# Gate and up products of a routed feed-forward: the token rows are held and the weights are moved, and the activations are transposed afterwards

## The chip, the cores and the metric

The kernel runs on one core of a Trainium2 chip. Its engines work side by side: TensorE (PE, matrix products, with its weight loads listed as PEld), VectorE (DVE), ScalarE (ACT), GpSimd (POOL) and SyncE (SP), which only issues transfers here. They hand work to each other by semaphores. The metric is the device time of one execution in microseconds (us), lower is better.

## The reference

Tokens `x` (32 batches of 112 rows of 256) first get a gated cross-attention over a context. The part that matters here comes after it, a mixture of eight experts with two chosen for each token:

```python
x = x + jnp.tanh(g_xattn[0]) * attention(...)
h = layernorm(x)
bids = jax.nn.sigmoid(h @ conf_w.T + conf_b) * wealth
top_bids, chosen = jax.lax.top_k(bids, 2)            # 2 of 8 experts
combine = sum(one_hot(chosen) * softmax(top_bids)[..., None], axis=2)
def ffn(gw, uw, dw):                                  # gw, uw 1024x256, dw 256x1024
    g = h @ gw.T
    u = h @ uw.T
    return (silu(g) * u) @ dw.T
out = x + jnp.tanh(g_ffn[0]) * einsum("ebsh,bse->bsh", all_ffn(h), combine)
```

The products have to be near fp32 precision. The kernel splits each fp32 operand into a high and a low fp16 part, and forms hi\*hi, hi\*lo and lo\*hi, so that each logical product is three passes of fp16.

## The kernel before

**Stages.** Until about 880 us the program does the attention for all batches, and routes: each token's normalised row is scattered twice, once for each chosen expert, into `routed_rows` in DRAM, which is sorted by expert. The second stage takes this table in tiles of P = 128 rows. There are NT = 63 tiles; a table `t_exp_i`, computed on VectorE after tile 0, gives the expert's place for each tile. Everything this case touches is in the second stage.

**One tile.** `xt` (128 rows x 256) is loaded by GpSimd's queue (`load_tile`, line 547), transposed by TensorE into `xP` (`tile_T`, line 1558), and split into `xT` high (ACT, `tile_hi`, line 842) and low (DVE, `tile_lo`, line 1302). Gate and up have 1024 outputs each, done in two halves i = 0, 1 of 512. `gate_up(t, q, i, slot)` forms `gP[i]` and `uP[i]` (one PSUM bank each). In the kernel before, each half of each of the two is four blocks of 128 outputs; a block is a `product` (line 1383, the helper that issues all fp16 products) of KD = 2 depth blocks by three parts, six matmuls. In each the *weights* are the stationary operand (128x128) and the *rows* `xT` move (128 columns). So the outputs come out with the features on the partitions, ready to be the stationary operand of the next product, and one bank takes 24 matmuls and 24 weight loads.

ACT then forms `sg` = silu(gate) (`silu`, line 848), DVE `act_h` = up \* constant \* sg (`gated`, line 1308), ACT the high part `aT[..][0]` (`act_hi`, line 854) and DVE the low part `aT[..][1]` (`act_lo`, line 1313). `down(t)` holds `aT` and moves the down weights in 256 columns, 24 matmuls into `yP`; DVE scales the rows (`weigh`, line 1320) into `ysb`, and GpSimd adds them to the output by a scattering, accumulating DMA (`add_tile`, line 598).

**Order of the work.** It is written out by hand in one `step(t, k)` for each engine, and each engine keeps its order:

- TensorE: `gate_up(t, 0)`, `tile_T(t + 1)`, on one tile in five `expert_sums`, `gate_up(t, 1)`, then a register load of the next tile's place (`place_of`), `down(t - 1)`, and the waits for the next tile's weights.
- ACT: `silu(t, 0)`, `act_hi(t, 0)`, `tile_hi(t + 1)`, `silu(t, 1)`, `act_hi(t, 1)`, then work on a later expert.
- DVE: `gated(t, 0)`, `act_lo(t, 0)`, `tile_lo(t + 1)`, `gated(t, 1)`, `act_lo(t, 1)`, `weigh(t - 1)`, then work on a later expert.
- GpSimd: waits until the add of tile t - 2 has landed, loads `xt` of tile t + 2, then adds tile t - 1.

The work on later experts belongs to tiles 0 to 34, five for each expert p = 1 to 7: in the first three ACT squares two pieces of 1024 raw weight columns each (`expert_squares`, line 796), in the last two ACT and DVE split three pieces each into high and low (`expert_hi` line 806, `expert_lo` line 1167). In the fourth, DVE also computes the expert's scale in a chain of small operations, with a power on GpSimd within it (lines 1149 to 1162). GpSimd loads the raw pieces in `load_raw` (line 510). Four expert slots lie in SBUF as `W2`; places 4 to 7 are split into a fifth, stored to DRAM by ACT's queue (line 812) and reloaded by SP's (line 397) when a slot is free.

The slot of a tile is a register from tile 3 on: `weights_of(byte, ...)` addresses `W2` by that register plus a constant. In tiles 0 to 2 the byte is a Python constant. The semaphore `s_there` tells TensorE that a slot is loaded; for the first four places SP raises it by hand, in the kernel before at line 410, behind its last transfers of the first stage.

Of the kernel before, what the change touches and what calls it, by code (L numbers as in the profile page):

```python
# [11 lines left out]
ACT = mybir.ActivationFunctionType  # L12
# [42 lines left out]
AHEAD = 4  # L55
assert AHEAD * P * E <= 2 * (TOK - 8 * S)
RELOADS = 4
X_TOP = 2.0 ** 10
A_TOP = 2.0 ** -21
SPAN = 5  # L60
# [21 lines left out]
def build(nc, x, ctxt, mask, scal, lnw, wqkv, wout, confw, confbw, wffn, out):  # L82
# [4 lines left out]
    with ctx:  # L87
        def sem(name):
            return ctx.enter_context(nc.semaphore(name))
# [4 lines left out]
        def psum(name, shape, stack):  # L94
            return stack.enter_context(nc.psum_tensor(name, shape, F32))
# [153 lines left out]
        yP = psum("yP", [P, 2, D], ppb)[:, 0, :]  # L249
        bP = psum("bP", [P, 512], ppb)  # L250
        uP = [psum(f"uP{i}", [P, 512], ppb) for i in range(2)]
        ppb.close()
        pb.close()

# [34 lines left out]
        s_xt = [sem(f"s_xt{i}") for i in range(4)]  # L289
        s_xtp, s_xthi, s_xtlo, s_gu, s_silu, s_act = [sem(n) for n in (  # L290
            "s_xtp", "s_xthi", "s_xtlo", "s_gu", "s_silu", "s_act")]
        s_athi, s_atlo, s_down, s_yw, s_add = [sem(n) for n in (
            "s_athi", "s_atlo", "s_down", "s_yw", "s_add")]

        def need(eng, semaphore, count):

# [11 lines left out]
        def seq(b, n):  # L308

            if isinstance(b, int) and b > B - 3 and n >= PK:  # L310
                n -= KD
            return b * NPIECE + (PRO + n)

        def zseq(b, k):

            return k if isinstance(b, int) and b == 0 else seq(b - 2, PZ + k)

        def in_place(p):

# [13 lines left out]
        def _(sp):  # L333
# [38 lines left out]
            def load_raw(p):  # L372

                e = sp.value_load(order_i[0:1, p:p + 1], min_val=0, max_val=E - 1)
                for c in range(PIECES):
                    need(sp, s_wlo, (p - 1) * PIECES + c + 1)
                    sp.dma_start(raw[:, piece_cols(c)],  # L377
                                 wffn[bass.ds(e, 1), :, piece_cols(c)].rearrange("a p c -> (a p) c")).then_inc(s_raw[c], 16)

            for b in range(8):  # L380
                turn_of(b, b % 2)
            with sp.Fori(4, B // 2) as g:
# [24 lines left out]
            load_raw(1)  # L407
            turn_of(B + 4, 0)

            sp.sem_inc(s_there, 16 * RELOADS * SLOTS)  # L410
            sp.wait_ge(s_tab, 1)
            for n in range(SLOTS, E):

# [218 lines left out]
        def _(act):  # L632
# [211 lines left out]
            def silu(t, i, place):  # L844

                act.wait_ge(s_gu, t * 2 + (i + 1))
                need(act, s_act, (t - 1) * 2 + (i + 1))
                nc.scalar.activation(sg[i][:, :], gP[i][:, :], ACT.Silu, scale=constant(place, 0)).then_inc(s_silu, 1)  # L848

            def act_hi(t, q, i):  # L850

                act.wait_ge(s_act, t * 2 + (i + 1))
                need(act, s_down, t)
                nc.scalar.activation(aT[q][i][:, 0, :, :].rearrange("p m s -> p (m s)"), act_h[i][:, :], ACT.Copy).then_inc(s_athi, 1)  # L854

            def step(t, k):
                q = k % 2
                if t < NT:
                    if t == 3:
                        act.wait_ge(s_tab, 1)  # L860
                    place = place_of(t)
                    silu(t, 0, place)
                    act_hi(t, q, 0)
                if t < NT - 1:
                    tile_hi(t + 1, 1 - q)
                if t < NT:
                    silu(t, 1, place)
                    act_hi(t, q, 1)
                p, j = t // SPAN + 1, t % SPAN
                if p < E:  # L870
                    if j < 3:
                        for c in (2 * j, 2 * j + 1):
                            expert_squares(p, c)
                    else:
                        for c in range((j - 3) * 3, (j - 2) * 3):
                            expert_hi(p, c)
                if SLOTS < p <= E and j == 0:
                    put_place(p - 1)

            tile_hi(0, 0)  # L880
            for t in range(NT):
                step(t, t % 4)

        @block.vector
        def _(dve):
# [419 lines left out]
            def gated(t, i, place):  # L1305

                dve.wait_ge(s_silu, t * 2 + (i + 1))
                nc.vector.scalar_tensor_tensor(out=act_h[i][:, :], in0=uP[i][:, :], scalar=constant(place, 2), in1=sg[i][:, :],  # L1308
                                               op0=ALU.mult, op1=ALU.mult).then_inc(s_act, 1)

            def act_lo(t, q, i):
                dve.wait_ge(s_athi, t * 2 + (i + 1))
                nc.vector.tensor_tensor(aT[q][i][:, 1, :, :].rearrange("p m s -> p (m s)"), act_h[i][:, :],  # L1313
                                        aT[q][i][:, 0, :, :].rearrange("p m s -> p (m s)"), ALU.subtract).then_inc(s_atlo, 1)

            def weigh(t, k, place):
# [5 lines left out]
            def step(t, k, place, last_place):  # L1322
                q = k % 2
                p, j = t // SPAN + 1, t % SPAN
                if t < NT:
                    gated(t, 0, place)
                    act_lo(t, q, 0)
                if t < NT - 1:
                    tile_lo(t + 1, 1 - q)
                if p < E and j == 3:  # L1330
                    expert_bound(p, bP)
                if t < NT:
                    gated(t, 1, place)
                    act_lo(t, q, 1)
                if p < E and j == 3:
                    expert_scale(p)
                if t > 0:
                    weigh(t - 1, (k - 1) % 4, last_place)
                if p < E and j >= 3:
                    for c in range((j - 3) * 3, (j - 2) * 3):  # L1340
                        expert_lo(p, c)
# [34 lines left out]
        def _(pe):  # L1376
# [194 lines left out]
            def gate_up(t, q, i, slot_):  # L1571

                if i == 0:
                    pe.wait_ge(s_xtlo, t + 1)
                need(pe, s_act, (t - 1) * 2 + (i + 1))
                for o, w in ((gP[i], WG), (uP[i], WU)):
                    for m in range(IB // 2):
                        col = w + (i * (IB // 2) + m) * P
                        last = product(o[:, m * P:(m + 1) * P], lambda k, a: weights_of(slot_, a, col + k * I, P),
                                       lambda k, a: xT[q][:, a, k, :], KD)  # L1580
                last.then_inc(s_gu, 1)

            def down(t, q, slot_):

# [14 lines left out]
            def step(t, k, byte, last_byte):  # L1599

                q = k % 2
                if t < NT:
                    gate_up(t, q, 0, byte)
                if t < NT - 1:
                    tile_T(t + 1, (k + 1) % 4)
                if t // SPAN + 1 < E and t % SPAN == 3:
                    expert_sums(t // SPAN + 1, bP)
                if t < NT:
                    gate_up(t, q, 1, byte)
                place = next_byte = None  # L1610
                if t == 2:
                    pe.wait_ge(s_tab, 1)
                if t < NT - 1:
                    place = place_of(t + 1)
                    next_byte = byte_of(place)
                if t > 0:
                    down(t - 1, 1 - q, last_byte)
                if t < NT - 1:
                    weights_there(place)
                return next_byte  # L1620
# [44 lines left out]
```

## Time and profile before

| | |
|---|---|
| median of 3 runs | 1584.86 us (1583.99 to 1586.45) |
| profiled execution, own time | 1586.34 us |
| profiled execution, span of the trace | 1584.7 us |
| mean granted TensorE clock | 0.984 |
| busy: PE, PEld, DVE, ACT, POOL | 91%, 69%, 66%, 59%, 30% |
| second stage, first gate product to the last down product | 880.74 to 1572.39 us |

The span is the time from the first to the last instruction of the trace, and the execution's own time has a little around it. The busy share of PE counts the time in which at least one matmul is under way. Matmuls are pipelined, so that the duration of one tells its latency and not its rate: a rate is read from the start of a run of matmuls to the start of the next run. In a row of the timeline, "x24" is 24 instructions merged, and the bracket tells how long the engine sat idle before, and for what ("issue" is an idle time that no semaphore in the profile explains).

### The profile page before, as it was taken

To read this page: it belongs to the slowest core of one execution; us is meant where nothing else is said; L and a number is where in the kernel's file an instruction comes from. 1 tells how busy PE (TensorE), PEld (TensorE's weight loads), DVE (VectorE), ACT (ScalarE), POOL (GpSimd) and SP (SyncE) were. 2 spreads that over 40 slices of the span, in tenths; PEclk is the share of its full clock that TensorE was granted. 3 is DMA by queue.
4 is the path that set the end of the run, shared out by engine and by line. 5 is a ranking of instruction groups with operands and counts; after the bars stand their busy time and mean duration, and the time that the engine had idled before them with its cause. 6 is when DMAs were issued, how large, how long until landed. Compare 5 with 4: busy or idle time off the path is not lost. (4 is left out here: it accounts for less than half of the span.)

```text
span 1584.7 us, 46877 instructions
## 1 busy us (share of the span) xinstructions
PE 1439.6 (91%) x15896; PEld 1096.9 (69%) x15896; DVE 1046.5 (66%) x2552; ACT 942.0 (59%) x1940; POOL 475.9 (30%) x644
## 2 busy tenths in 40 slices
PE   1999999999999999999996799999998999999996
PEld 1566666666666666666665788888787888888875
DVE  4688898898988989889877555445435533333332
ACT  4678777787878778787867454545445422222221
POOL 4232224334243342432413332233222212212211
PEclk9999999999999999999996899999999999999999
DMA  3011011111111010110122542333357231111351
GB/s 114 18 38 38 27 38 42 44 36 50 37 39 50 27 58 24 50 45 29 38 93 75 160 108 38 93 108 120 89 184 237 52 105 26 26 28 26 105 187 15
DMA packets 52198, 107.49 MB, mean 68 GB/s; under 512 B 10704, under 2 KB 32592, under 8 KB 51472
## 3 DMA queue, kind: packets, MB, share of 16 engines
q0 software_dynamic: 20448, 43.13, 11.4%
q1 hardware_dynamic: 29824, 46.70, 9.8%
q10 hardware_dynamic: 1712, 14.70, 2.5%
q8 instruction: 148, 2.42, 0.6%
q14 instruction: 66, 0.54, 0.1%
HBM read 69.16 MB, written 35.34 MB: 66 GB/s over the span
## 5 line engine op out<-in xcount | busy, mean ns | idle before, releaser
L1308 DVE SCALAR_TENSOR_TENSOR act_h<-uP,consts,sg 128x512 f32<-128x512 f32 x126 | 94.6, 751 | 253.0 <-ACT sg L848 252.7
L848 ACT ACTIVATE sg<-gP,consts 128x512 f32<-128x512 f32 x126 | 86.5, 687 | 280.1 <-PE uP L1383 280.0
L1383 PE MATMUL uP<-xT,W 128*128 128x128 f16 x3024 | 250.0, 217 | 0.9
L1383 PE MATMUL fP<-zTs,ws 128*128 128x112 f16 (+1 forms) x1536 | 221.2, 295 | 10.5 <-POOL zTs L479 8.9
L1383 PEld LDWEIGHTS uP<-xT,W 128*128 (+1 forms) x3024 | 209.5, 96 | 29.5 <-issue 4.7
L1383 PE MATMUL gP<-xT,W 128*128 128x128 f16 x3024 | 223.7, 218 | 5.6 <-DVE xT L1302 3.2
L1383 PE MATMUL yP<-W,aT 128*128 (+1 forms) x1512 | 179.3, 275 | 44.8 <-issue 43.9
L1383 PEld LDWEIGHTS gP<-xT,W 128*128 (+1 forms) x3024 | 202.1, 97 | 22.6 <-issue 7.9
L1383 PEld LDWEIGHTS yP<-W,aT 128*128 128x128 f16 x1512 | 144.4, 98 | 71.4 <-issue 52.8
L598 POOL DMA_INDIRECT out<-ysb,xt x63 | 105.2, 1669 | 287.9 <-DVE ysb L1320 266.6
L702 ACT ACTIVATE pr<-ms,nmax 112x488 f32<-112x488 f32 x256 | 179.0, 699 | 15.9 <-DVE nmax L948 14.3
L1383 PE MATMUL fP<-ws,zTs 128*128 128x512 f16 x768 | 187.0, 379 | 0.2
L948 DVE CUSTOM_DVE_ANT_0 ms<-simP,madd,sim_undo 112x488 f32<-112x488 f32 x256 | 184.1, 719 | 3.1 <-PE simP L1431 0.8
L1383 PEld LDWEIGHTS fP<-zTs,ws 128*128 128x128 f16 x1536 | 110.0, 99 | 102.2 <-issue 38.1
L954 DVE SCALAR_TENSOR_TENSOR pT<-ptP,pT 122x448 f16<-122x448 f32 x256 | 158.0, 617 | 20.9 <-ACT pT L709 19.9
L709 ACT ACTIVATE pT<-ptP 122x448 f16<-122x448 f32 x256 | 137.8, 538 | 39.9 <-PE ptP L1441 38.6
L1383 PE MATMUL oP<-v,pT 122*128 122x64 f16 x3072 | 133.5, 194 | 20.4 <-DVE pT L954 17.6
L854 ACT ACTIVATE aT<-act_h 128x512 f16<-128x512 f32 x126 | 79.3, 630 | 118.3 <-DVE act_h L1308 118.3
L1313 DVE TENSOR_TENSOR aT<-act_h,aT 128x512 f16<-128x512 f32 x126 | 87.2, 692 | 87.7 <-ACT aT L854 87.7
L1441 PE MATMUL ptP<-ident,pr 112*122 112x112 f32 x1024 | 142.6, 262 | 0.5 <-DVE filled L1059 0.5
L1383 PEld LDWEIGHTS oP<-v,pT 122*128 122x128 f16 x3072 | 122.7, 98 | 28.9 <-DVE pT L954 28.8
L1441 PEld LDWEIGHTS ptP<-ident,pr 112*122 112x122 f32 x1024 | 115.2, 140 | 25.2 <-issue 1.2
(210 smaller groups left out, 2119.0 us busy)
## 6 DMA issues: line engine op xcount, KB each, us to landing
raw<-wffn POOLq DMA_DIRECT2D x36, 512.0 KB, 7.2
split_experts<-W ACTq DMA_DIRECT2D x4, 3072.0 KB, 10.4
W<-split_experts SPq DMA_DIRECT2D x16, 768.0 KB, 8.0
xc<-ctxt SPq DMA_DIRECT2D x32, 375.0 KB
xt<-routed_rows POOLq DMA_DIRECT2D x63, 129.0 KB, 2.4
raw<-wffn SPq DMA_DIRECT2D x12, 512.0 KB, 9.0
xl<-x SPq DMA_DIRECT2D x32, 112.0 KB
xres<-x SPq DMA_DIRECT2D x32, 112.0 KB, 4.8
```

The lines of the kernel that those rows point to most:

```text
L598: pool.indirect_dma_start(out[:, :], bass.IndirectOffsetOnAxis(ap=xt[k][:, D:D + 1].bitcast(I32), axis=0), ysb[k % 2][:, :], None, compute ...
L702: nc.scalar.activation(pr[h % 2][:, :], ms[h % 2][:, :], ACT.Exp, bias=nmax[p][:, h:h + 1], scale=-1.0, accum_out=rsum[p][:, h:h + 1]).the ...
L709: nc.scalar.activation(pT[h % 2][:, 0, :, 0:S], ptP[h % 2][0:KR, :, 0:S], ACT.Copy, scale=P_TOP).then_inc(s_pthi, 1)
L848: nc.scalar.activation(sg[i][:, :], gP[i][:, :], ACT.Silu, scale=constant(place, 0)).then_inc(s_silu, 1)
L854: nc.scalar.activation(aT[q][i][:, 0, :, :].rearrange("p m s -> p (m s)"), act_h[i][:, :], ACT.Copy).then_inc(s_athi, 1)
L948: nc.vector.tensor_tensor_reduce(out=ms[h % 2][:, :], in0=simP[h % 2][0:S, 0:NK], in1=madd[p][:, :], scale=sim_undo[0:S, 0:1], scalar=3.0e ...
L954: nc.vector.scalar_tensor_tensor(out=pT[h % 2][:, 1, :, 0:S], in0=ptP[h % 2][0:KR, :, 0:S], scalar=P_TOP, in1=pT[h % 2][:, 0, :, 0:S], op0 ...
L1308: nc.vector.scalar_tensor_tensor(out=act_h[i][:, :], in0=uP[i][:, :], scalar=constant(place, 2), in1=sg[i][:, :], op0=ALU.mult, op1=ALU.mu ...
L1313: nc.vector.tensor_tensor(aT[q][i][:, 1, :, :].rearrange("p m s -> p (m s)"), act_h[i][:, :], aT[q][i][:, 0, :, :].rearrange("p m s -> p ( ...
L1383: last = nc.tensor.matmul(o, lhs(k, a), rhs(k, c), start=n == 0, stop=n == len(todo) - 1)
L1441: last = nc.tensor.transpose(ptP[h % 2][0:KR, c, 0:S], pr[h % 2][:, c * KR:(c + 1) * KR], ident[0:S, 0:S])
```

## The change

In `gate_up` the operands change places for both halves (`TURNED = (0, 1)`): the 128 rows are the stationary operand and the weights move, 512 columns at once. A bank takes six matmuls in place of 24. The outputs then come with the rows on the partitions, `act_h` too. So a new `act_T(t, i)` on TensorE transposes `act_h[i]` in four blocks of 128 (fp32, against `ident`) into a new PSUM bank `aP`, one for both halves. `act_hi` and `act_lo` read `aP` in place of `act_h`. The bank is used in turn: the transposes of a half wait until `act_lo` of the half before is done, and `gated` waits until the transposes of the tile before have read `act_h`.

The order changes with it. TensorE's step becomes `gate_up(t, 0)`, `act_T(t - 1, 1)`, `tile_T(t + 1)`, `expert_sums`, `gate_up(t, 1)`, the place, `act_T(t, 0)`, `down(t - 1)`. ACT's becomes `silu(t, 0)`, `act_hi(t - 1, 1)`, `tile_hi(t + 1)`, `silu(t, 1)`, `act_hi(t, 0)`; DVE's `gated(t, 0)`, `act_lo(t - 1, 1)`, `tile_lo(t + 1)`, `gated(t, 1)`, `act_lo(t, 0)`, `weigh(t - 1)`. The second half of a tile is thus made ready in the next step. SP's raising of `s_there` moves to the start of its program.

```diff
--- before.py
+++ after.py
@@ -55,6 +55,7 @@
 AHEAD = 4
 assert AHEAD * P * E <= 2 * (TOK - 8 * S)
 RELOADS = 4
+TURNED = (0, 1)
 X_TOP = 2.0 ** 10
 A_TOP = 2.0 ** -21
 SPAN = 5
@@ -249,6 +250,7 @@
         yP = psum("yP", [P, 2, D], ppb)[:, 0, :]
         bP = psum("bP", [P, 512], ppb)
         uP = [psum(f"uP{i}", [P, 512], ppb) for i in range(2)]
+        aP = psum("aP", [P, 512], ppb)
         ppb.close()
         pb.close()
 
@@ -289,8 +291,8 @@
         s_xt = [sem(f"s_xt{i}") for i in range(4)]
         s_xtp, s_xthi, s_xtlo, s_gu, s_silu, s_act = [sem(n) for n in (
             "s_xtp", "s_xthi", "s_xtlo", "s_gu", "s_silu", "s_act")]
-        s_athi, s_atlo, s_down, s_yw, s_add = [sem(n) for n in (
-            "s_athi", "s_atlo", "s_down", "s_yw", "s_add")]
+        s_at, s_athi, s_atlo, s_down, s_yw, s_add = [sem(n) for n in (
+            "s_at", "s_athi", "s_atlo", "s_down", "s_yw", "s_add")]
 
         def need(eng, semaphore, count):
 
@@ -314,6 +316,10 @@
         def zseq(b, k):
 
             return k if isinstance(b, int) and b == 0 else seq(b - 2, PZ + k)
+
+        def turned(t, i):
+
+            return t * len(TURNED) + TURNED.index(i) + 1
 
         def in_place(p):
 
@@ -377,6 +383,7 @@
                     sp.dma_start(raw[:, piece_cols(c)],
                                  wffn[bass.ds(e, 1), :, piece_cols(c)].rearrange("a p c -> (a p) c")).then_inc(s_raw[c], 16)
 
+            sp.sem_inc(s_there, 16 * RELOADS * SLOTS)
             for b in range(8):
                 turn_of(b, b % 2)
             with sp.Fori(4, B // 2) as g:
@@ -407,7 +414,6 @@
             load_raw(1)
             turn_of(B + 4, 0)
 
-            sp.sem_inc(s_there, 16 * RELOADS * SLOTS)
             sp.wait_ge(s_tab, 1)
             for n in range(SLOTS, E):
 
@@ -849,9 +855,13 @@
 
             def act_hi(t, q, i):
 
-                act.wait_ge(s_act, t * 2 + (i + 1))
+                if i in TURNED:
+                    act.wait_ge(s_at, turned(t, i))
+                else:
+                    act.wait_ge(s_act, t * 2 + (i + 1))
                 need(act, s_down, t)
-                nc.scalar.activation(aT[q][i][:, 0, :, :].rearrange("p m s -> p (m s)"), act_h[i][:, :], ACT.Copy).then_inc(s_athi, 1)
+                src = aP if i in TURNED else act_h[i]
+                nc.scalar.activation(aT[q][i][:, 0, :, :].rearrange("p m s -> p (m s)"), src[:, :], ACT.Copy).then_inc(s_athi, 1)
 
             def step(t, k):
                 q = k % 2
@@ -860,12 +870,16 @@
                         act.wait_ge(s_tab, 1)
                     place = place_of(t)
                     silu(t, 0, place)
-                    act_hi(t, q, 0)
+                if t > 0:
+                    act_hi(t - 1, 1 - q, 1)
                 if t < NT - 1:
                     tile_hi(t + 1, 1 - q)
                 if t < NT:
+                    if 0 not in TURNED:
+                        act_hi(t, q, 0)
                     silu(t, 1, place)
-                    act_hi(t, q, 1)
+                    if 0 in TURNED:
+                        act_hi(t, q, 0)
                 p, j = t // SPAN + 1, t % SPAN
                 if p < E:
                     if j < 3:
@@ -878,7 +892,7 @@
                     put_place(p - 1)
 
             tile_hi(0, 0)
-            for t in range(NT):
+            for t in range(NT + 1):
                 step(t, t % 4)
 
         @block.vector
@@ -1305,12 +1319,17 @@
             def gated(t, i, place):
 
                 dve.wait_ge(s_silu, t * 2 + (i + 1))
+                if i in TURNED:
+                    need(dve, s_at, turned(t - 1, i))
+                else:
+                    need(dve, s_atlo, (t - 1) * 2 + (i + 1))
                 nc.vector.scalar_tensor_tensor(out=act_h[i][:, :], in0=uP[i][:, :], scalar=constant(place, 2), in1=sg[i][:, :],
                                                op0=ALU.mult, op1=ALU.mult).then_inc(s_act, 1)
 
             def act_lo(t, q, i):
                 dve.wait_ge(s_athi, t * 2 + (i + 1))
-                nc.vector.tensor_tensor(aT[q][i][:, 1, :, :].rearrange("p m s -> p (m s)"), act_h[i][:, :],
+                src = aP if i in TURNED else act_h[i]
+                nc.vector.tensor_tensor(aT[q][i][:, 1, :, :].rearrange("p m s -> p (m s)"), src[:, :],
                                         aT[q][i][:, 0, :, :].rearrange("p m s -> p (m s)"), ALU.subtract).then_inc(s_atlo, 1)
 
             def weigh(t, k, place):
@@ -1324,14 +1343,18 @@
                 p, j = t // SPAN + 1, t % SPAN
                 if t < NT:
                     gated(t, 0, place)
-                    act_lo(t, q, 0)
+                if t > 0:
+                    act_lo(t - 1, 1 - q, 1)
                 if t < NT - 1:
                     tile_lo(t + 1, 1 - q)
+                if t < NT and 0 not in TURNED:
+                    act_lo(t, q, 0)
                 if p < E and j == 3:
                     expert_bound(p, bP)
                 if t < NT:
                     gated(t, 1, place)
-                    act_lo(t, q, 1)
+                    if 0 in TURNED:
+                        act_lo(t, q, 0)
                 if p < E and j == 3:
                     expert_scale(p)
                 if t > 0:
@@ -1574,12 +1597,25 @@
                     pe.wait_ge(s_xtlo, t + 1)
                 need(pe, s_act, (t - 1) * 2 + (i + 1))
                 for o, w in ((gP[i], WG), (uP[i], WU)):
+                    if i in TURNED:
+                        col = w + i * 512
+                        last = product(o[:, :], lambda k, a: xT[q][:, a, k, :],
+                                       lambda k, a: weights_of(slot_, a, col + k * I, 512), KD)
+                        continue
                     for m in range(IB // 2):
                         col = w + (i * (IB // 2) + m) * P
                         last = product(o[:, m * P:(m + 1) * P], lambda k, a: weights_of(slot_, a, col + k * I, P),
                                        lambda k, a: xT[q][:, a, k, :], KD)
                 last.then_inc(s_gu, 1)
 
+            def act_T(t, i):
+
+                pe.wait_ge(s_act, t * 2 + (i + 1))
+                need(pe, s_atlo, t * 2 + i)
+                for m in range(IB // 2):
+                    last = nc.tensor.transpose(aP[:, m * P:(m + 1) * P], act_h[i][:, m * P:(m + 1) * P], ident[:, :])
+                last.then_inc(s_at, 1)
+
             def down(t, q, slot_):
 
                 pe.wait_ge(s_atlo, t * 2 + 2)
@@ -1601,6 +1637,8 @@
                 q = k % 2
                 if t < NT:
                     gate_up(t, q, 0, byte)
+                if t > 0:
+                    act_T(t - 1, 1)
                 if t < NT - 1:
                     tile_T(t + 1, (k + 1) % 4)
                 if t // SPAN + 1 < E and t % SPAN == 3:
@@ -1613,6 +1651,8 @@
                 if t < NT - 1:
                     place = place_of(t + 1)
                     next_byte = byte_of(place)
+                if t < NT and 0 in TURNED:
+                    act_T(t, 0)
                 if t > 0:
                     down(t - 1, 1 - q, last_byte)
                 if t < NT - 1:
```

## Rows read from the trace of the kernel before

**Rows 1.** Page, part 2: TensorE clock granted in 40 slices of the span.

```profile
PEclk9999999999999999999996899999999999999999
```

**Rows 2.** Chain that ended last, whole span: start us, us, what.

```profile
936.60 2.78 PE yP L1383 x24
...
1555.60 2.79 PE yP L1383 x24
```

**Rows 3.** Timeline of one steady tile: start us, us, engine, line, operation [idle before].

```profile
1434.37 2.78 PE L1383 MATMUL yP<-W,aT 128*128 x24 [0.69 <-issue]
...
1436.99 1.63 PE L1383 MATMUL gP<-xT,W 128*128 128x128 f16 x24
1437.31 0.54 DVE L1320 TENSOR_SCALAR ysb<-yP,xt,consts 128x256 f32<-128x256 f32 x1 [0.74 <-PE yP L1383]
...
1438.51 2.14 PE L1383 MATMUL uP<-xT,W 128*128 128x128 f16 x24
1438.72 1.60 POOL L598 DMA_INDIRECT out<-ysb,xt  x1 [5.20 <-DVE ysb L1320]
...
1440.57 0.41 PE L1558 MATMUL xP<-ident,xt 128*128 128x128 f32 x2
...
1440.79 0.69 ACT L848 ACTIVATE sg<-gP,consts 128x512 f32<-128x512 f32 x1 [4.94 <-PE uP L1383]
1440.81 1.87 PE L1383 MATMUL gP<-xT,W 128*128 128x128 f16 x24
1441.63 0.75 DVE L1308 SCALAR_TENSOR_TENSOR act_h<-uP,consts,sg 128x512 f32<-128x512 f32 x1 [3.78 <-ACT sg L848]
1442.42 0.63 ACT L854 ACTIVATE aT<-act_h 128x512 f16<-128x512 f32 x1 [0.94 <-DVE act_h L1308]
...
1443.08 0.69 DVE L1313 TENSOR_TENSOR aT<-act_h,aT 128x512 f16<-128x512 f32 x1 [0.70 <-ACT aT L854]
...
1445.28 2.78 PE L1383 MATMUL yP<-W,aT 128*128 x24 [0.66 <-issue]
```

**Rows 4.** Timeline of tiles 1 and 2.

```profile
899.89 1.50 PE L1383 MATMUL gP<-xT,W 128*128 128x128 f16 x24 [2.58 <-DVE xT L1302]
...
902.79 1.50 PE L1383 MATMUL gP<-xT,W 128*128 128x128 f16 x24
...
904.13 1.50 PE L1383 MATMUL uP<-xT,W 128*128 128x128 f16 x24
```

**Rows 5.** Timeline of TensorE in the attention stage.

```profile
507.86 2.64 PE L1383 MATMUL fP<-zTs,ws 128*128 128x488 f16 x12
...
510.34 0.55 PE L1441 MATMUL ptP<-ident,pr 112*122 112x112 f32 x4
...
510.73 0.52 PE L1383 MATMUL oP<-v,pT 122*128 122x64 f16 x12
```

**Rows 6.** Groups by line, 900 to 1560 us: busy us, mean ns of one.

```profile
L1167 DVE SCALAR_TENSOR_TENSOR W<-raw,escale,W 128x1024 f16<-128x1024 f32 x42 | 51.4, 1279 | 0.0
...
L796 ACT ACTIVATE junk<-raw 128x1024 bf16<-128x1024 f32 x40 | 42.0, 1049 | 7.8 <-DMA raw<-wffn 6.2
```

**Rows 7.** Timeline, tile 3: end of the scale chain on VectorE.

```profile
918.80 0.17 DVE L1155 TENSOR_SCALAR ebits<-epow 128x3 int32<-128x3 int32 x1 [0.78 <-POOL epow L502]
...
920.04 0.55 DVE L1320 TENSOR_SCALAR ysb<-yP,xt,consts 128x256 f32<-128x256 f32 x1
```

**Rows 8.** Timeline of GpSimd around the first store of a split expert.

```profile
1105.31 1.64 POOL L598 DMA_INDIRECT out<-ysb,xt  x1 [4.86 <-DVE ysb L1320]
...
1116.44 0.54 POOL L547 DMA_DIRECT2D xt<-routed_rows  x1 [7.58 <-issue]
```

**Rows 9.** Page, part 6: DMA issues, KB each, us to landing.

```profile
raw<-wffn POOLq DMA_DIRECT2D x36, 512.0 KB, 7.2
...
xt<-routed_rows POOLq DMA_DIRECT2D x63, 129.0 KB, 2.4
```

**Rows 10.** DMA landing of the scatter-adds of line 598, us.

```profile
DMA to landing us min/median/max: 3.7/3.9/9.7
```

## The prediction

> **What bounds the kernel now.** I read the chain of waits first, for what limits the stage that the change touches, then the timeline of one tile, then the rows of the other engines to see what covers what. In the chain, the second stage is TensorE from end to end: the down product of tile 4 starts at 936.60 and that of tile 60 at 1555.60 [rows 2], so 56 tiles take 619.0 us, 11.05 each. The granted clock is at its upper level, 2.4 GHz, in all of these slices [rows 1].
>
> One steady tile shows what they consist of [rows 3]. Take starts, not durations: down 1434.37 to 1436.99, 2.62 us; gate and up of half 0 until 1440.57, 3.58; transposing the next rows until 1440.81, 0.24; half 1 until the next down at 1445.28, 4.47, of which 0.66 is idle ("issue"). The sum is 10.91. The other engines wait: ScalarE stood idle 4.94 us before its silu. The 56 tiles hold (11.05 - 10.91) x 56 = 8 us of irregular stalls besides.
>
> A bank's 24 matmuls are not at the array's rate. In tile 2 the gate bank started at 902.79 and the up bank at 904.13 [rows 4], 1.34 us or 56 ns a matmul; in the steady tile a bank takes 1.8 to 2.1 us, 75 to 86 ns. The code says what differs: from tile 3 the weights' address is a register. I read this as TensorE's instruction stream (48 instructions a bank, with address arithmetic) being slower than the array, which leaves nothing queued ahead; so the register load of the next place, behind half 1, shows as the 0.66 us of idle. Down has as many matmuls but twice the columns, and runs at 2.62 / 24 = 109 ns, its array rate.
>
> **The change part by part.**
>
> *Gate and up.* 96 matmuls with their loads go, 24 of 512 columns come. The nearest row is an attention product: 12 matmuls of 488 columns from 507.86 to 510.34 [rows 5], 207 ns each, so 217 ns for 512. The 24 cost 5.21 us a tile, against 3.58 + 3.81 = 7.39. A weight load is hidden under 512 columns. The dynamic operand is now the moving one, as down's is already. The Trainium skill, "TensorE: Matmul & The Clock Gate", section "Back-to-back issue gap", gives about 131 ns a matmul for a stream of loads and 512-column matmuls; that would make the 24 cost 3.1 us and the total some 115 us lower. The trace contradicts it with 207 ns for 488 columns, and I take the trace.
>
> *The place load.* The stream of half 1 becomes 12 matmuls that occupy the array for 2.6 us, and even at 86 ns a pair they are issued in about 1.0 us. The load then lies beside the array's work: 0.66 us goes. Bounds: 0 and 0.66 kept.
>
> *Transposes.* Eight fp32 ones a tile are added. Two of `xP` take 0.24 us from start to start [rows 3], 120 ns each; four of 112 columns took 0.39 us, 510.34 to 510.73 [rows 5]. Eight cost 0.96 us. Upper bound: not overlapped, one takes 0.41 - 0.12 = 0.29 us [rows 3], eight 2.3 us.
>
> *TensorE's tile* is then 5.21 + 0.96 + 0.24 + 2.62 = 9.03 us, 1.88 less. 56 tiles: 505.7 in place of 619.0.
>
> *The waits of `act_T(t, 0)`*, with down and the next gate queued behind it. It needs `act_lo(t - 1, 1)`, second in VectorE's step. From the end of half 0: hand-over 0.14 and silu 0.69, gated until 1.73, as in [rows 3] (1440.65, 1440.79, 1441.63). ScalarE's high part (0.63) fits between 0.85 and 1.5, since the transposes of the other half are done at about 0.8; VectorE's low part (0.69) ends near 2.45. TensorE arrives at 0.48 + 0.24 + 2.60 = 3.3. Slack 0.9 us: no stall in a plain tile. The new reads are from PSUM where SBUF was read; both engines read banks already at similar cost (gated 0.75 us), and I take no difference, at worst 0.1 us, inside the slack.
>
> *Split tiles.* That slack is what the work on later experts eats. VectorE has three pieces of 1.28 us [rows 6] behind `weigh` in two tiles of five. In the fourth of five it also waits for the power and runs the scale chain, 0.78 us idle and 1.24 us from `ebits` to `ysb` [rows 7]. From the end of half 1: low part 2.3, chain 4.3, weigh 4.85, three pieces 8.6, gated 9.35, low part 10.05; TensorE wants it at 9.03. About 1 us, 7 times: 7 us. The plain split tile comes out even.
>
> *Raw pieces.* GpSimd issues them behind the add, 3 to 5 us after the end of down; the median landing is 7.2 us [rows 9], so the second lies there at about 12. ScalarE would want the first at about 7.4 in the shorter tile, squares two (1.05 us each [rows 6] and 0.19 to read the sum), and its next silu is due at 11.8. It comes some 2 us late, 1.2 beyond the slack: 6 experts x 1.2, and 2 us more in each of the four tiles where a split expert is being stored: 15 us. Before, these waits were hidden but for 6.2 us on ScalarE alone.
>
> *Rows of the next tiles.* The load of tile t + 2 waits until the add of tile t - 2 has landed. The add starts 1.73 us after the end of down (1436.99, 1438.72 [rows 3]); TensorE wants the rows one tile and a half later: 10.91 + 3.58 - 1.73 = 12.8 us after the add's start before, 9.03 + 3.1 - 1.73 = 10.4 after. Ordinarily the add lands in 3.9 [rows 10] and the load in 2.4 [rows 9], ample. Beside 3 MB transfers they don't: from 1105.31 the next load could start only at 1116.44 [rows 8], 11.1 us, 13.5 with its landing, so 3.1 late. The trace has seven such distances, 8.4 to 11.1, and one of 7.7 with a landing of 6.1: together 16 us late. Of the 8 us of stalls that are there, I keep 5 beside these.
>
> *Start and end.* Tiles 0 to 2 already ran at the array's rate, so each gains nothing and pays 0.96 us. The down of tile 0 now waits for `act_lo(0, 1)`, which stands behind the table chain on VectorE (TensorE idled 2.58 us there already [rows 4]): some 2.5 us more. Tile 3 wins back part, and down of tile 4 starts about 1.6 us earlier than now. SP's earlier signal gives 0.4 us at most, in this. At the end, the last half's transposes, high and low parts stand alone before the last down, 1 us longer; the two last tiles win about as much. Zero.
>
> *Sum*: 505.7 + 7 + 15 + 16 + 5 = 549 in place of 619, -70; -1.6 at the start: **-72 us**. Against the profiled execution's own 1586.3 us that is 1514.5; the median of the runs shown is 1.5 us lower than this execution, so **1513**.
>
> **Rivals.**
>
> *The cover holds better*: no late pieces and rows. The floor is 1586.3 - 113 - 2 = 1471; half the 38 us of late work gives 1494. For: the engines get long idle times. Against: the waits above are ordered by program, not by load. 0.2.
>
> *The gap survives*: the place load stalls TensorE before `act_T(t, 0)` instead. 0.66 x 57 = 38 us: 1551. For: in the down of [rows 3] it stands behind a full half. Against: that half was issue-bound. 0.08.
>
> *Split tiles don't gain*: each of 31 keeps 10.9 and only 25 gain 1.88: 1586 - 47, with some late rows, about 1545. 0.08.
>
> *Transposes at full price*: 0.29 us each, 8 x 0.17 x 57 = 78 us: 1591, no change. For: none overlapped with a 512-column neighbour in this trace. Against: both rows of pairs and fours. The skill's same page, Part 4, has a PE-mode transpose at about 275 ns in a kernel, and says that it doesn't engage the fast clock; the trace agrees with the single duration, not with the rate, and shows no clock drop from the `xP` ones. 0.04.
>
> *The one bank becomes the path, slower*: the place is TensorE at `act_T(t, 0)`, waiting for the low part of the half before, with down behind it. It decides where the hand-overs take over 0.9 + 1.27 = 2.2 us more than I read, 1.27 being what is left of the 72 us on each of 57 tiles. At 3 us more it costs 0.83 x 57 = 47 us net: 1633. Against: every piece of that path has a row. 0.05.
>
> **How the numbers follow.** Forecast 0.55, then 0.2, 0.08, 0.08, 0.04, 0.05. The range 1482 to 1552 holds the forecast's own (raw and row waits from half to twice), most of the first rival, and the next two. A measurement of this kernel can tell about 0.2%, 3 us, from no change. Slower are the last rival and part of full-price transposes, 0.06; within 3 us 0.03; faster 0.91.
>
> **What would show it.** In the profile after: 6 matmuls of a bank in 1.30 us from start to start; four transposes in 0.48; no idle before down; plain tiles at 9.0 to 9.1 us in the last 25; idle before transposes of rows waiting for DMA, 16 us in sum, and before `aP` transposes waiting for VectorE or ScalarE in the split tiles, 22 us. It would be wrong if banks took over 1.5 us, if the clock row fell below 9 in these slices, or if plain tiles took over 9.5.

## The result, and the profile after

The changed kernel takes 1499.23 us (median of 4 runs, 1496.08 to 1499.66) where the kernel before took 1585.39 (4 runs, 1583.99 to 1586.45): ratio 0.9453, 95% interval 0.9436 to 0.9469, 86 us less. The profiled execution is the fastest of the four, 1496.08 us with a span of 1494.5.

The page of the changed kernel, parts 1 and 2 (busy us and share, instructions; clock granted in 40 slices):

```profile
PE 1372.3 (92%) x11864; PEld 899.9 (60%) x11864; DVE 1034.9 (69%) x2552; ACT 925.8 (62%) x1940; POOL 475.6 (32%) x644
...
PEclk9999999999999999999999969999999999999999
```

TensorE lost 4032 matmuls and as many loads, net of the transposes, but its busy share rose from 91% to 92%: it is the bound still. The 6 in the clock row is the slice from 859 to 897 us, ahead of the stretch that is compared below. The down products of tiles 4 and 60, from TensorE's timeline, stand against [rows 2]:

```profile
934.44 2.78 PE L1406 MATMUL yP<-W,aT 128*128 x24
...
1466.82 2.78 PE L1406 MATMUL yP<-W,aT 128*128 x24
```

56 tiles take 532.4 us, 9.51 each, in place of 619.0 and 11.05. The two profiled executions lie 90 us apart (1586.34 and 1496.08), and these 87 us are all of that but 4. The chain of waits over two plain tiles shows what one consists of, against [rows 3]:

```profile
1384.25 2.62 PE yP L1406 x24
1386.87 1.29 PE gP L1406 x6
1388.17 1.29 PE uP L1406 x6
1389.46 0.44 PE aP L1616 x4
1389.90 0.22 PE xP L1581 x2
1390.12 1.29 PE gP L1406 x6
1391.41 1.29 PE uP L1406 x6
1392.71 0.44 PE aP L1616 x4
1393.14 2.62 PE yP L1406 x24
```

A bank is 1.29 us, 216 ns a matmul; four transposes are 0.44, 109 ns each; down is 2.62 as before; and nothing idle stands before down. From down to down it is 8.89 us, and in the last 25 tiles nearly every one has this length. 56 of them make 498 us, so 35 us of the stretch are something else. Nine tiles take 9.6 to 16.2 us and hold 30 of these 35. One of them, in the timeline of all engines:

```profile
1074.22 0.35 ACTq L818 DMA_DIRECT2D split_experts<-W  x1
...
1074.36 1.64 POOL L604 DMA_INDIRECT out<-ysb,xt  x1 [3.03 <-DVE ysb L1339]
...
1086.43 1.06 ACT L802 ACTIVATE junk<-raw 128x1024 bf16<-128x1024 f32 x1 [5.19 <-DMA raw<-wffn]
...
1086.77 0.55 POOL L553 DMA_DIRECT2D xt<-routed_rows  x1 [9.11 <-issue]
...
1089.76 0.69 PE L1581 MATMUL xP<-ident,xt 128*128 128x128 f32 x2 [4.68 <-DMA xt<-routed_rows]
...
1090.24 2.77 PE L1406 MATMUL gP<-W,xT 128*128 x6
...
1092.80 2.40 PE L1406 MATMUL uP<-W,xT 128*128 x6
...
1095.04 0.60 PE L1616 MATMUL aP<-ident,act_h 128*128 128x128 f32 x4
```

ScalarE's queue has just begun to store a split expert (3 MB, at 1074.22). The add that started at 1074.36 is done so late that GpSimd loads the next rows only at 1086.77, and TensorE stands 4.68 us before their transposes. In the same tile ScalarE waited 5.19 us for a raw piece, but it was done before the rows were there. Then the gate bank takes 2.56 us and the up bank 2.24: the granted clock was 0.53 of full from 1090 to 1095, nearly all of it at the lower of the two levels (1.2 GHz), and 1.00 in the tiles before the stall. So this stall costs 7 us where its idle time is 4.7. There are four such stalls, of 2.9 to 4.7 us, one after each of the four stores. The clock fell in each of them or right behind it, and the slow products after them cost some 8 us together. These rows of the table of waits name what TensorE and ScalarE waited for (us in total, times, longest), from 870 us to the end:

```profile
ACT junk L802 <- DMA raw<-wffn: 23.8, 13, 5.2
...
PE xP L1581 <- DMA xt<-routed_rows: 19.9, 9, 4.7
...
PE aP L1616 <- DVE aT L1332: 4.3, 5, 3.2
```

The 4.3 us on VectorE are one wait of 3.2 at the stage's start, and 1.1 us in all of the split tiles. ScalarE's wait for raw pieces grew from 6.2 [rows 6] to 23.8 us, but hardly reached TensorE.

### The profile page after: what moved, and what is told of

It reads as the page before. It is cut to its first block and busy times, and to the rows that moved or that the text cites. A ratio compares the mean times of both kernels' runs of the same rounds, so it can differ in the third digit from the quotient of the medians.

```text
span 1494.5 us, 36175 instructions
## 1 busy us (share of the span) xinstructions
PE 1372.3 (92%) x11864; PEld 899.9 (60%) x11864; DVE 1034.9 (69%) x2552; ACT 925.8 (62%) x1940; POOL 475.6 (32%) x644
## 5 line engine op out<-in xcount | busy, mean ns | idle before, releaser
L1406 PE MATMUL gP<-W,xT 128*128 (+1 forms) x756 | 189.7, 388 | 1.6 <-DVE xT L1316 1.6
L1406 PE MATMUL uP<-W,xT 128*128 (+1 forms) x756 | 187.5, 385 | 0.0
L1406 PEld LDWEIGHTS yP<-W,aT 128*128 128x128 f16 x1512 | 148.7, 98 | 18.9 <-issue 1.7
L1406 PEld LDWEIGHTS uP<-W,xT 128*128 128x128 f16 x756 | 75.1, 99 | 93.1 <-issue 6.8
L485 POOL TENSOR_TENSOR zTs<-zT,zTs 128x1200 f16<-128x1200 f32 x32 | 79.2, 2474 | 157.5 <-ACT zTs L689 157.4
L1406 PEld LDWEIGHTS fP<-ws,zTs 128*128 128x128 f16 x768 | 68.0, 98 | 82.0 <-issue 14.4
L1406 PEld LDWEIGHTS gP<-W,xT 128*128 128x128 f16 x756 | 75.2, 100 | 66.5 <-issue 7.0
```

Source lines behind the costliest of these rows:

```text
L485: nc.gpsimd.tensor_tensor(zTs[p][:, 1, :, :], zT[:, :, :], zTs[p][:, 0, :, :], ALU.subtract).then_inc(s_zsplit, 1)
L1406: last = nc.tensor.matmul(o, lhs(k, a), rhs(k, c), start=n == 0, stop=n == len(todo) - 1)
```

## The experiments

The kernels of the experiments ran on three other chips, in three groups of four. There the first stage takes longer in either kernel (the first gate product of the changed one starts at 906.36 us in place of 879.53), and the kernel before has medians of 1616.9, 1617.2 and 1616.1 us. The second stage doesn't differ: the stretch from the down of tile 4 to that of tile 60 is 534.0 us there (e5) and 532.4 on the first chip. I call this **the stretch** and compare by it, and by ratios to the kernel before on the same chip.

### Why the old banks were slow (e1, e2, e3)

```diff
             def byte_of(place):
 
-                return place % SLOTS * (2 * WCOL * 2)
+                return 0
...
-                    sp.dma_start(W2[:, n % SLOTS, :, c * step_:(c + 1) * step_],
+                    sp.dma_start(W2[:, max(1, n % SLOTS), :, c * step_:(c + 1) * step_],
```

> The kernel before, but TensorE takes the weights of every tile from slot 0 by a constant address (places 1 to 7 use the wrong weights; SP reloads into slots 1 to 3 only, the same bytes). Theory A: before was bound by TensorE's instruction stream, 96 register-addressed matmul and load pairs a tile. Then a bank takes 1.34 us from start to start as in tiles 0 to 2, the 0.66 us of idle before down goes since the queue is filled, a plain tile takes 4 x 1.34 + 0.24 + 2.62 = 8.2 us, and the whole is some 1470 us. Rival B: 128 moving columns under a 128-column load are slow in the array itself: banks stay at 1.8 to 2.1 us and the time at 1585 us.

Measured: 1511.15 us, one run; the stretch 519.9 us. The timeline of one tile of e1:

```profile
1403.21 1.50 PE L1383 MATMUL gP<-xT,W 128*128 128x128 f16 x24
1404.55 1.50 PE L1383 MATMUL uP<-xT,W 128*128 128x128 f16 x24
1405.89 0.39 PE L1558 MATMUL xP<-ident,xt 128*128 128x128 f32 x2
1406.11 1.50 PE L1383 MATMUL gP<-xT,W 128*128 128x128 f16 x24
1407.45 1.50 PE L1383 MATMUL uP<-xT,W 128*128 128x128 f16 x24
1408.79 2.78 PE L1383 MATMUL yP<-W,aT 128*128 128x256 f16 x24
```

Every bank starts 1.34 us after the one before, the idle before down is gone, and a plain tile takes 8.20 us, as theory A said; B falls. The products are as many and of the same shapes as in the kernel before; only where their weights lie differs (and so the output, since all tiles take the weights of place 0). So the array can do 128 columns in 56 ns a matmul, and what was slow is the instruction stream with a register in each address. In `weights_of` an offset is added to that register for each address, and e1 takes away both, the register operand and the addition; no run tells them apart. The whole is 41 us above the 1470 that I gave, of which about 30 are this chip's first stage; the other 10 are stalls: the stretch holds 61 us beside its plain tiles, and TensorE waits 38.8 us in all for rows. The old orientation, where it is not bound by the stream, is 0.69 us a tile faster than the new one.

In e2 the changed kernel moves its weights in blocks of 128 columns, and in e3 of 256:

```diff
                     if i in TURNED:
-                        col = w + i * 512
-                        last = product(o[:, :], lambda k, a: xT[q][:, a, k, :],
-                                       lambda k, a: weights_of(slot_, a, col + k * I, 512), KD)
+                        for m in range(512 // 128):
+                            col = w + i * 512 + m * 128
+                            last = product(o[:, m * 128:(m + 1) * 128], lambda k, a: xT[q][:, a, k, :],
+                                           lambda k, a: weights_of(slot_, a, col + k * I, 128), KD)
                         continue
```

> The changed kernel with its moving weights cut into blocks of 128 columns: 24 matmuls and 24 loads a bank as before the change, but the register address is on the matmul and not on the load. Theory A (any register operand costs the stream the same): banks back at 1.8 to 2.0 us, gap of some 0.6 us before the transposes of half 0, plain tile about 11.5 us, whole some 1650 us. Rival C (only a register on the weight load is slow): banks at 1.34 us, plain tile 9.1 us, whole 1505 to 1510 us.

> The same with blocks of 256 columns, 12 matmuls and 12 loads a bank. Theory A: 12 x 85 ns = 1.0 us of stream lie under 12 x 109 ns = 1.31 us of array, so a bank takes 1.31 us, a plain tile about 8.95 us, the whole 1498 to 1503 us. A theory by which the gain is in proportion to the number of instructions saved expects about a third of it back, 1525 us.

Measured: e2 1633.23 us, stretch 634.7; e3 1531.75 us, stretch 538.5 (one run each, kernel before 1616.9). TensorE in e2, and then in e3:

```profile
1400.25 0.63 PE L1617 MATMUL aP<-ident,act_h 128*128 128x128 f32 x4 [0.51 <-issue]
...
1403.33 1.50 PE L1406 MATMUL gP<-W,xT 128*128 x24
1404.67 2.14 PE L1406 MATMUL uP<-W,xT 128*128 x24
1406.67 0.63 PE L1617 MATMUL aP<-ident,act_h 128*128 128x128 f32 x4
```

```profile
1403.37 1.47 PE L1406 MATMUL gP<-W,xT 128*128 x12
1404.68 1.47 PE L1406 MATMUL uP<-W,xT 128*128 x12
1405.99 0.60 PE L1617 MATMUL aP<-ident,act_h 128*128 128x128 f32 x4
```

With 24 matmuls a bank, the up banks take 2.0 us again, and the idle time is back, 0.5 us, now before the transposes of half 0. Only the first bank after down, 1.34, is at the array's rate; I read this as work that was queued while down ran. It doesn't matter whether the register is on the load or on the matmul: rival C falls. Holding the rows gains nothing by itself; with 128 columns the changed kernel is slower than the one before, as it has the transposes to pay. With 256 columns a bank takes 1.31 us, a plain tile 8.95, and nearly everything is gained that 512 gain: once the stream is faster than the array, fewer instructions bring no more.

### What the order and the signal are worth (e4, e12)

e4 is the changed kernel with `TURNED = ()` and no `act_T`:

```diff
-TURNED = (0, 1)
+TURNED = ()
...
-                if t > 0:
+                if t > 0 and 1 in TURNED:
                     act_T(t - 1, 1)
```

> The new order of the work (second half's high and low parts one step later, SP's early signal) with the old gate and up products and without transposes. Theory: TensorE is the bound and the order only moves work beside it, so 1585 us within 4 us. Rival D: part of the gain came from the order: then 1570 us or less.

Measured: 1615.59 us (10 runs), ratio 0.9987 (0.9976 to 0.9999) and stretch 618.3 us: the order alone, with the old products, brings at most a quarter of a per cent. D falls. What the new products would take in the old order was not run.

e12 puts SP's `sem_inc` of `s_there` back behind its last transfers.

> The changed kernel with SP's signal for the first four slots where it was before the change. Theory: the first gate product then waits for SP as before, 1.2 us (880.74 against 879.53 us in the two traces of the first chip), and all after it stays; rival: no wait seen, since VectorE's part of the rows comes last anyway.

Measured: 1527.67 us, one run; stretch 531.4. Its low part of the rows on VectorE, and its first product:

```profile
910.65 0.42 DVE L1316 SCALAR_TENSOR_TENSOR xT<-xP,xT 128x256 f16<-128x256 f32 x1
...
911.51 2.72 PE L1406 MATMUL gP<-W,xT 128*128 128x512 f16 x6 [1.91 <-SPq L416]
```

Both were half right. SP is what came last, but only just: the product starts 0.44 us after the low part, where it was 0.14 in the changed kernel. The signal is worth 0.3 us. The 1.2 us that I read from two traces was mostly that the first stage had ended 0.9 us sooner in one of them.

### What the transposes cost (e9, e10)

```diff
-                for m in range(IB // 2):
+                for m in list(range(IB // 2)) * 2:
                     last = nc.tensor.transpose(aP[:, m * P:(m + 1) * P], act_h[i][:, m * P:(m + 1) * P], ident[:, :])
```

> The changed kernel with each block of the activations transposed twice into the same place, 16 transposes a tile. Theory: they lie on TensorE's path at about 109 ns each (0.436 us for four, as the changed kernel shows), so a plain tile goes from 8.89 to 9.76 us and the 56 tiles gain 40 to 49 us over the changed kernel's 532 to 534. Rival: hidden beside other work, no change; or at 0.29 us each, 11.2 us a plain tile.

Measured: 1557.53 us, one run; stretch 560.8. Eight in a row, and where the rows' transposes start behind them:

```profile
1404.55 1.04 PE L1616 MATMUL aP<-ident,act_h 128*128 128x128 f32 x8
1405.43 0.38 PE L1581 MATMUL xP<-ident,xt 128*128 128x128 f32 x2
```

Eight take 0.88 us, and a plain tile 9.77: the transposes are wholly on the path, at 110 ns each. But the stretch grew by 27 us and not by 40 to 49. 56 plain tiles are 547 of it, so that only 14 us of stalls are left, where e5 has 36. TensorE waits 8.2 us for rows here, in e5 22.0. I read this as the longer tile giving the rows more time to come: of the 49 us that the transposes cost, 22 were paid out of the stalls.

e10 holds the rows for half 1 alone:

```diff
-TURNED = (0, 1)
+TURNED = (1,)
```

> Only half 1 holds the rows (TURNED = (1,)); half 0 is as before the change. Theory A gives a plain tile by its parts: half 0 3.58, transposes 0.44, rows 0.22, half 1 2.59, no idle before down since its stream is short, down 2.62: 9.45 us. A rival, by which the idle of 0.66 us before down belongs to the register load and not to the stream: 10.1 us.

Measured: 1518.32 us, one run; stretch 528.8. My sum failed here, on the good side. TensorE over a plain tile, down to down:

```profile
1400.11 1.50 PE L1406 MATMUL gP<-xT,W 128*128 128x128 f16 x24
1401.45 1.67 PE L1406 MATMUL uP<-xT,W 128*128 128x128 f16 x24
1403.03 0.63 PE L1616 MATMUL aP<-ident,act_h 128*128 128x128 f32 x4
1403.49 0.38 PE L1581 MATMUL xP<-ident,xt 128*128 128x128 f32 x2
1403.71 1.46 PE L1406 MATMUL gP<-W,xT 128*128 x6
1405.01 1.46 PE L1406 MATMUL uP<-W,xT 128*128 x6
1406.30 2.78 PE L1406 MATMUL yP<-W,aT 128*128 x24
1408.92 1.50 PE L1406 MATMUL gP<-xT,W 128*128 128x128 f16 x24
```

The tile is 8.81 us, 0.08 *less* than with both halves turned. Half 0 takes 2.92 us and not 3.58: its gate bank runs at the array's rate (1.34), its up bank nearly (1.58). What stands before them, the turned half and down, is long in the array and short in the stream, so I take it that much of half 0 is already queued when it begins; the timeline doesn't show the queue. Four transposes, 0.44 us, are saved. By this the stream need only keep up over the tile, not in each bank. The whole is 0.939 of the kernel before on its chip, in one run, where e5 has 0.9445 of it on another.

### The stalls (e5 to e8, e11)

e6 takes six row buffers, indexed by the tile, and loads rows ahead of the wait for the add:

```diff
+                if holds(t, AHEAD - 3, NT - 4):
+                    load_tile(t + 3, (k + 3) % 4)
                 if holds(t, 2, NT):
                     pool.wait_ge(s_add, t * 16 - 16)
                     apart(pool)
-                if holds(t, AHEAD - 2, NT - 3):
-                    load_tile(t + 2, (k + 2) % 4)
```

e7 moves `add_tile` in GpSimd's step behind both `load_raw`. e8 has both, and calls `tile_table()` on VectorE in step 1, ahead of `weigh(0)`, and not behind step 0. e11 has the first two, six buffers and raw pieces first.

> The changed kernel as it is, beside the three below on one chip. Its 56 tiles from the down of tile 4 to that of tile 60 take 532 us (9.51 each) again, within 4 us, of which 498 are plain tiles of 8.89 us and some 30 lie in the nine tiles that wait for rows; ratio to the kernel before 0.945 to 0.948.

> The changed kernel with six row buffers in place of four, and the rows of tile t + 3 loaded ahead of the wait for the add of tile t - 2, not those of tile t + 2 behind it. Theory E: the stalls left are rows that come late because that add lands in up to 11 us beside the 3 MB transfers, and the clock that falls in those stalls. Then no tile takes over 11 us, the idle before the transposes of rows (20 us) is nearly gone, and the time is 22 to 30 us below the changed kernel. Rival F: the transfers would stall TensorE in another place (the scaled rows' buffers, the raw pieces): less than 10 us gained.

> The changed kernel with GpSimd's loads of raw weight pieces ahead of its add, not behind it: some 5 us earlier. Theory: ScalarE's 24 us of waiting for raw pieces fall to under 5, TensorE wins 3 to 8 us, since most of that wait was inside the slack. Rival G: the pieces now run beside the load of the rows and the add, and the row waits grow by as much or more.

> Six row buffers, raw pieces first, and the tile table computed in step 1 behind act_lo instead of behind step 0. Theory: the gains add, -25 us for the rows, -5 for the pieces, -3 for the table: 33 us below the changed kernel, 0.925 of the kernel before. The 56 tiles take about 503 us.

> Six row buffers and raw pieces first, the table where the change has it. Theory: the table's place is worth 2.8 us at the start of the stage and nothing later, so the 56 tiles take the 503 us of the three together, and the whole 1496 us on this chip, ratio 0.925 to 0.927. Rival: the table's place mattered for the later collisions too, then over 6 us slower than the three together.

| | us (runs) | ratio to before | the stretch |
|---|---|---|---|
| e5, changed, again | 1526.84 (4) | 0.9445 (0.9429 to 0.9460) | 534.0 |
| e6, six row buffers | 1502.96 (4) | 0.9292 (0.9273 to 0.9311) | 510.1 |
| e7, raw first | 1533.74 (1) | | 540.6 |
| e8, three together | 1493.41 (4) | 0.9234 (0.9215 to 0.9253) | 502.7 |
| e11, rows and raw | 1496.89 (4) | 0.9261 (0.9246 to 0.9276) | 503.1 |

e6 gains 24 us, and no wait for rows is left: theory E holds, but not wholly. Three tiles still take 11.2 to 12.3 us. What ends their waits is another thing, in the timeline of e6:

```profile
1115.17 1.06 ACT L803 ACTIVATE junk<-raw 128x1024 bf16<-128x1024 f32 x1 [6.01 <-DMA raw<-wffn]
...
1118.54 0.63 PE L1617 MATMUL aP<-ident,act_h 128*128 128x128 f32 x4 [2.74 <-DVE aT L1333]
```

ScalarE waited 6.01 us for a raw piece, with its silu queued behind, and TensorE then 2.74 us for the low part. In the changed kernel such waits (5.2, 5.2 and 3.9 us of ScalarE) lay under the longer ones for rows, in the same three tiles. The three stalls of TensorE in e6 are 2.1, 2.7 and 3.2 us long, and the granted clock stayed at 1.00 around each of them.

e7 alone did as rival G said. ScalarE doesn't wait for raw pieces any more, but TensorE waits 29.6 us for rows in place of 22.0, and the stretch is 6.6 us longer. In e11, where the rows don't depend on the add, the same edit takes 7 us off the stretch of e6. e8 then is 33 us below the changed kernel, as expected. What is left of ScalarE's wait for raw pieces, from its table of waits:

```profile
ACT junk L803 <- DMA raw<-wffn: 7.1, 2, 4.9
```

From the first gate product to the down of tile 4, e8 takes 51.8 us, e5 54.6, e6 54.7, e11 55.7: the table's place is worth about 3 us there and nothing after. e8 is faster than both kernels of the case.

e8 with one half turned, as in e10, was not tried; nor were experiments that keep the slot's address constant with correct weights.

## Why the prediction was right, and where not

The forecast was 72 us less. The profiled executions lie 90 us apart and the medians 86; 1499 is within the range, 14 us below the 1513. By its steps:

- **What bounds the kernel.** Right: the stream of instructions, shown by e1. The 0.66 us of idle before down was the same thing; it goes in e1 with the register load of the place still there. One reading was off: a bank of the steady tile was said to take 1.8 to 2.1 us, but the gate bank behind down takes 1.52 [rows 3], 63 ns a matmul from start to start. The sum went by 3.58 us for the half and doesn't need it.
- **Gate and up, transposes, down.** 9.03 us forecast, 8.89 measured, 8 us in 56 tiles. The bank's 217 ns a matmul came out as 216; the eight transposes were 0.87 us and not 0.96, and the two of `xP` 0.22 and not 0.24. All go at 109 to 110 ns each here; why two took 0.24 in the kernel before is open.
- **The waits of `act_T(t, 0)`.** Right in plain tiles: no such wait in any of the last 25.
- **Split tiles.** 7 us forecast, 1.1 us of waiting measured. The timeline of the changed kernel, VectorE and TensorE, in a fourth tile of five (half 1 of the tile before ends at 1207.45):

```profile
1211.13 0.54 DVE L1339 TENSOR_SCALAR ysb<-yP,xt,consts 128x256 f32<-128x256 f32 x1 [0.16 <-DVE consts L1176]
...
1215.83 0.68 DVE L1332 TENSOR_TENSOR aT<-aP,aT 128x512 f16<-128x512 f32 x1
...
1216.66 0.63 PE L1616 MATMUL aP<-ident,act_h 128*128 128x128 f32 x4 [0.15 <-DVE aT L1332]
```

The scaled rows start 3.7 us after the half and not 4.3, for the power was ready and the 0.78 us of [rows 7] didn't come again. The low part ends 9.1 us after the half, where the forecast had 10.05, and TensorE stood 0.15 us.

- **Raw pieces.** 15 us forecast, about none seen. ScalarE did wait 23.8 us, and where the row waits are gone (e6) 8 us of TensorE's stalls are for them, half of the term. What failed above all is the adding up: both stalls fall in the same tiles, beside the same transfers, and the longer one hides the shorter.
- **Rows of the next tiles.** 16 us forecast, 20 measured, and 8 more that no step had: the clock after a stall. The prediction took the clock to be at its upper level throughout the stage, by a row of tenths [rows 1]. But the timeline of the kernel before already had two falls, at 1113 and 1226 us, each at an idle time of under 2 us:

```profile
1112.97 4.45 PE L1383 MATMUL yP<-W,aT 128*128 x24 [1.84 <-issue]
1117.26 1.50 PE L1383 MATMUL gP<-xT,W 128*128 128x128 f16 x24
```

That down product took 4.29 us, the other 4.25, in place of 2.62, at a granted clock of 0.60. The 5 us kept for other stalls are there still: what the named waits and the clock leave of the 34.6 us is 5.5, small pieces spread over the tiles.
- **Start and end.** 1.6 us forecast for the start, 2.2 measured (1.0 without the first stage's own 1.2). The down of tile 0 waited for the low part behind the table, as forecast, and again the clock made it dearer:

```profile
896.31 0.71 PE L1616 MATMUL aP<-ident,act_h 128*128 128x128 f32 x4 [3.22 <-DVE aT L1332]
896.82 4.41 PE L1406 MATMUL yP<-W,aT 128*128 128x256 f16 x24
901.06 1.46 PE L1406 MATMUL gP<-W,xT 128*128 128x512 f16 x6
```

That product took 4.24 us and not 2.62. The end gained 1.4 us where I gave zero.

The sum of the misses: 8 for the tile, 8.5 for stalls (43 forecast, 34.6 measured), 2 at the two ends, together 18 between the profiled executions. The three have the same sign, but within the stalls the signs differ: 15 and 6 less for pieces and split tiles, 4 more for rows and 8 more for the clock. That the stalls came out near their sum is in part luck. Of the signs that were named, the banks, the idle before down and the rows came as said; the plain tile was 8.89 and not 9.0 to 9.1, and the 22 us of idle before `aP` transposes were 1.1.

Of the rivals, "the cover holds better" has a time, 1494 with half of the late work, that is nearer to the measured 1499 than the forecast. Its cause holds for the pieces and split tiles and not for the rows, whose waits were longer than forecast; nearly half of the difference from the forecast is the shorter tile. The Trainium skill's 131 ns for a 512-column matmul in a stream, "TensorE: Matmul & The Clock Gate", section "Back-to-back issue gap", is not what this kernel shows: 216 ns. The 275 ns for a transpose that the Trainium skill gives on the same page, in Part 4, is the duration of one here (274 ns) and not the rate, 109 ns.

## What to carry to other kernels

Before you price a matmul by its columns, compare the rate of the same product with a constant and with a register address. If the stream is the bound, what pays is fewer instructions for the same array time, and only until the stream keeps up over the whole step, so that turning half of the work may be enough. When a bound engine gets faster, list the transfers that had an old step's time to land; of stalls that fall in the same tile the longest is taken, and not their sum. A stall of some microseconds on TensorE can be charged again by the clock, and its length alone doesn't tell whether it is. Removing one of two such waits can make the other worse, as e7 shows: try them together.

## What was not expected of the hardware

- In the changed kernel each stall of TensorE of 2.9 to 4.7 us was followed by one or two banks at 2.0 to 2.6 us in place of 1.3, with a granted clock of 0.50 to 0.53 behind three of the four. In the kernel before, idle times of 1.8 and 1.9 us went with such a fall; in e6, stalls of 2.1, 2.7 and 3.2 us did not.
- A matmul and load pair with a register address in one of the two goes out every 74 to 86 ns (banks of 1.8 to 2.1 us, in the kernel before and in e2). The gate banks behind down are faster, 63 ns in the kernel before and 56 in e2, and so is e2's behind the transposes, 61. With a constant address every pair of e1 takes 56 ns.
- Half 0 of e10, 48 pairs behind 5.2 us of long matmuls, ran at 56 to 66 ns a pair in spite of its register addresses.
- ScalarE reads PSUM faster than SBUF here: `act_hi` takes 588 ns from `aP` in the changed kernel and 630 from `act_h` in the one before; in e10, which has both, 587 and 629.
